# Decoder layer, attention stage: value projections moved into the position part and written by VectorE in the next block; first outputs normalised ahead of the last adds

## The reference, cut to what matters

```python
q, k, v = split_heads(x @ Wq + bq), split_heads(x @ Wk + bk), split_heads(x @ Wv + bv)   # 16 heads of 8
scores = einsum('bhqd,bhkd->bhqk', q, k) / scale
c2p = take_along_axis(einsum('bhqd,hpd->bhqp', q, pos_k), c2p_pos, -1)      # q against 64 position buckets
p2c = swapaxes(take_along_axis(einsum('bhkd,hpd->bhkp', k, pos_k), p2c_pos, -1), -1, -2)
probs = softmax(scores + (c2p + p2c) / scale)
out = einsum('bhqk,bhkd->bhqd', probs, v) @ Wo + bo + x
x = layernorm(x + layernorm(out) * ln_scale + ln_bias)
```

## Time and profile before

| | us |
|---|---|
| median of three runs | 2737.05 |
| the profiled execution's own time | 2735.33 |
| its span, first to last instruction | 2733.6 |
| TensorE busy | 2375.6 (87%) |
| ScalarE busy | 2270.4 (83%) |
| VectorE busy | 2129.8 (78%) |
| GpSimd busy | 577.6 (21%) |
| mean granted TensorE clock | 0.945 |

### The profile page before, as it was taken

The page is one execution under the profiler, slowest core; times in us unless marked ns, Lnnn a source line. Parts: engine busy times, 40 slices in busy tenths (PEclk is TensorE's granted clock), DMA queues, the critical chain, the costliest instruction groups (busy, mean ns, idle before and its releaser), DMA issues. The chain is left out here.

```text
span 2733.6 us, 64386 instructions
## 1 busy us (share of the span) xinstructions
PE 2375.6 (87%) x18133; PEld 1298.0 (47%) x18133; DVE 2129.8 (78%) x6451; ACT 2270.4 (83%) x4511; POOL 577.6 (21%) x435
## 2 busy tenths in 40 slices
PE   3888888888883478555999999999999999999997
PEld 2666665666662256233444444444444444444443
DVE  4778888788775766954788888888888888888886
ACT  2899999989993533266999999999999999999996
POOL 3233242332420011233111111111111111111114
PEclk6999999999996589876999999999999999999999
DMA  4231222312211000000111111111111111111112
GB/s 112 53 77 44 68 58 51 75 45 67 58 43 46 1 0 0 31 0 1 47 52 57 46 46 46 46 52 57 46 46 46 46 53 56 46 46 46 46 52 87
DMA packets 195627, 129.61 MB, mean 47 GB/s; under 512 B 26667, under 2 KB 184443, under 8 KB 195579
## 3 DMA queue, kind: packets, MB, share of 16 engines
q1 hardware_dynamic: 195579, 129.02, 17.9%
HBM read 78.10 MB, written 4.73 MB: 30 GB/s over the span
## 5 line engine op out<-in xcount | busy, mean ns | idle before, releaser
L2002 DVE TENSOR_TENSOR c_Hl<-c_HF,c_Hh 128x512 f16<-128x512 f32 x1028 | 679.4, 688 | 161.5 <-ACT c_Hh L1889 145.1
L1885 ACT ACTIVATE c_HF<-c_H,c_b 128x512 f32<-128x512 f32 x1028 | 710.6, 691 | 64.2 <-PE c_H L1824 44.0
L1889 ACT ACTIVATE c_Hh<-c_H,c_b 128x512 f16<-128x512 f32 x1028 | 706.2, 687 | 0.0
L1940 POOL TENSOR_TENSOR c_EX<-c_euler,c_D 128x16 f32<-128x16 f32 x65 | 188.7, 2902 | 1194.1 <-DVE c_D L1975 1194.1
L1823 PE MATMUL c_H<-c_Cl,SH 128*128 128x512 f16 x1028 | 390.2, 380 | 0.0
L1822 PE MATMUL c_H<-c_Ch,SH 128*128 128x512 f16 x1028 | 390.2, 380 | 0.0
L1824 PE MATMUL c_H<-c_Ch,SH 128*128 128x512 f16 x1028 | 390.0, 379 | 0.0
L1833 PE MATMUL c_Y<-c_Hh,SH 128*128 128x512 f16 x1024 | 388.1, 379 | 0.1
L1835 PE MATMUL c_Y<-c_Hl,SH 128*128 128x512 f16 x1024 | 388.1, 379 | 0.0
L1834 PE MATMUL c_Y<-c_Hh,SH 128*128 128x512 f16 x1024 | 388.1, 379 | 0.0
L649 ACT ACTIVATE a_E<-a_T,a_nm 128x128 f32<-128x128 f32 x1024 | 325.3, 395 | 27.6 <-DVE a_nm L741 26.2
(11 more groups left out here) (296 smaller groups left out, 4076.2 us busy)
## 6 DMA issues: line engine op xcount, KB each, us to landing
c_CWB<-c_rows SPq DMA_DIRECT2D x260, 256.0 KB, 4.0
a_AB<-a_ST SPq DMA_DIRECT2D x256, 128.0 KB, 2.4
a_QN<-a_QH SPq DMA_DIRECT2D x128, 32.0 KB, 1.9
a_KN<-a_KH SPq DMA_DIRECT2D x128, 32.0 KB, 1.9
out<-d_O SPq DMA_DIRECT2D x16, 256.0 KB, 2.3
a_QN<-a_QL SPq DMA_DIRECT2D x64, 32.0 KB, 1.9
a_KN<-a_KL SPq DMA_DIRECT2D x64, 32.0 KB, 1.9
CUR<-in_ctx SPq DMA_DIRECT2D x1, 1848.0 KB
```

Source lines behind the costliest of these rows:

```text
L1885: act.activation(HF[:, k % 4, :], bH[k % 4][:, :], ACT.Gelu_apprx_tanh, bias=b1[:, g % EXPERTS, f:f + 1], scale=1.0 / WSCALE).then_inc(hf_ ...
L1889: act.activation(Hh[:, g % 2, f, :], bH[k % 4][:, :], ACT.Gelu_apprx_tanh, bias=b1[:, g % EXPERTS, f:f + 1], scale=1.0 / WSCALE).then_inc( ...
L2002: dve.tensor_tensor(Hl[:, g % 2, f, :], HF[:, k % 4, :], Hh[:, g % 2, f, :], ALU.subtract)\
```

## The change

The four value projections move from steps 10 to 13 to steps 20 to 23, behind the two chunks of each step, and write bank bO in place of bM. VN and GpSimd's copy `values_out` go. `values_in` moves from u = 14 to u = 1 of the next block, and writes V itself, from the bank. TensorE's wait for VN ahead of the first `out_transpose` goes. The first `softmax_outputs`, at u = 15, comes ahead of that step's `add_positions`. The four unread matmuls write bE[0] in place of bO. In the prologue a memset of ET and a matmul that filled bO with zeros go.

```diff
--- before.py
+++ after.py
@@ -39,9 +39,9 @@
 TAIL = CHUNKS // 2
 NORM_STEPS = (2, 3, 4, 5, 6, 7, 14)
 TILE_STEPS = (5, 6, 7, 8, 9, 10, 11, 12)
-V_STEPS = (10, 11, 12, 13)
+V_STEPS = (20, 21, 22, 23)
 C2P_MID, P2C_MID = 47, 17
-CONSTS, FILLS, TAB, BUILT = 13, 6, 10, 4
+CONSTS, FILLS, TAB, BUILT = 13, 5, 10, 4
 DVE_CHUNKS = tuple((c, 1) for c in range(1, CHUNKS))
 ACT_CHUNKS = tuple((c, f) for c in range(CHUNKS) for f in range(2) if (c, f) not in DVE_CHUNKS)
 EARLY_MAX = range(0, 0)
@@ -162,7 +162,6 @@
         ST = sb("ST", [P, 2, 2, S, NG, NB], F16)
         AB = sb("AB", [P, 2, 2, S, NG * NB], F16)
         POS = sb("POS", [P, 2, ROWX, S])
-        VN = sb("VN", [P, NB, NH, DH])
         V = sb("V", [P, NB, NH, VCOLS])
         OC = sb("OC", [P, 2, UPB, S])
         T = sb("T", [P, 3, HG, S])
@@ -205,8 +204,7 @@
             sem(n) for n in ("loaded", "late_in", "x_in", "consts", "filled"))
         tab_ps, tab, built = sem("tab_ps"), sem("tab"), sem("built")
 
-        xb, xT_ps, xT_ok, vn_ok, v_ok, kd_ok = (
-            Count(sem(n), 1) for n in ("xb", "xT_ps", "xT_ok", "vn_ok", "v_ok", "kd_ok"))
+        xb, xT_ps, xT_ok, v_ok, kd_ok = (Count(sem(n), 1) for n in ("xb", "xT_ps", "xT_ok", "v_ok", "kd_ok"))
         v_ps = Count(sem("v_ps"), NB)
         qk_ps, hi_ok, lo_ok = (Count(sem(n), 2) for n in ("qk_ps", "hi_ok", "lo_ok"))
         qn_in, kn_in = ([Count(sem(n + str(g)), 16 * 3) for g in range(NG)] for n in ("qn_in", "kn_in"))
@@ -332,12 +330,6 @@
                                               group_mask[:, h:h + 1], 1.0, ALU.mult, ALU.mult)
                 last.then_inc(kd_ok.sem, 1)
 
-            def values_out(i, nxt):
-                if nxt:
-                    hold(pool, spare_pool, pv.sem, pv.at(i, UNITS))
-                hold(pool, spare_pool, vn_ok.sem, vn_ok.at(i, 1 + nxt))
-                pool.tensor_copy(V[:, :, :, 0:DH], VN[:, :, :, :]).then_inc(v_ok.sem, 1)
-
             n = 2
 
             def const(ins):
@@ -375,12 +367,9 @@
             pool.memset(V[:, :, :, :], 0.0).then_inc(filled, 1)
             pool.wait_ge(filled, 4)
             pool.memset(V[:, :, :, DH:DH + 1], 1.0).then_inc(filled, 1)
-            pool.wait_ge(filled, 5)
-            pool.memset(ET[:, 0, :, :], 0.0).then_inc(filled, 1)
             pool.wait_ge(filled, FILLS)
             pool.wait_ge(built, BUILT)
             spread_keys(0, 0)
-            values_out(0, 0)
             def power(i, n):
                 pool.wait_ge(var_ok.sem, var_ok.at(i, n + 1))
                 pool.tensor_tensor(rstd[:, :], rstd[:, :], half[:, :], ALU.pow).then_inc(rstd_ok.sem, 1)
@@ -405,7 +394,6 @@
                 residuals(i, first)
                 if not last:
                     spread_keys(i, 1)
-                    values_out(i, 1)
 
             body(0, first=True)
             with pool.Fori(1, NBLK - 1) as i:
@@ -432,7 +420,7 @@
                 pe.matmul(bG[1][:, :], Wk[:, :], xT[:, :, :], start=True, stop=True).then_inc(qk_ps.sem, 1)
 
             def project_v(b):
-                pe.matmul(bM[:, b * S:(b + 1) * S], xT[:, :, b], Wv[:, :], start=True, stop=True).then_inc(v_ps.sem, 1)
+                pe.matmul(bO[:, b * S:(b + 1) * S], xT[:, :, b], Wv[:, :], start=True, stop=True).then_inc(v_ps.sem, 1)
 
             def bucket_tile(i, nxt, n):
                 kind, g = n // NG, n % NG
@@ -509,8 +497,6 @@
 
             def out_transpose(i, b, last):
                 pe.wait_ge(on_ok.sem, on_ok.at(i, b + 1))
-                if b == 0 and not last:
-                    pe.wait_ge(vn_ok.sem, vn_ok.at(i, 2))
                 if b == 0 and last:
                     pe.wait_ge(r_ok.sem, r_ok.at(i, 0))
                 pe.transpose(bM[:, b * S:(b + 1) * S], On[:, b % 2, :], ident[:, :]).then_inc(ot_ps.sem, 1)
@@ -548,7 +534,6 @@
             last.then_inc(tab_ps, 1)
             pe.wait_ge(built, BUILT)
             pe.wait_ge(filled, FILLS)
-            pe.matmul(bO[:, :], ident[:, :], ET[:, 0, :, :], start=True, stop=True)
             for n in range(TILES):
                 bucket_tile(0, 0, n)
             for c in range(CHUNKS):
@@ -572,8 +557,6 @@
                         project_q(i, 1)
                     if u == 2 and not last:
                         project_k()
-                    if u in V_STEPS and not last:
-                        project_v(V_STEPS.index(u))
                     for n in tiles_of(u):
                         if not last:
                             bucket_tile(i, 1, n)
@@ -586,9 +569,11 @@
                     if u >= UNITS and not last:
                         for c in (2 * (u - UNITS), 2 * (u - UNITS) + 1):
                             position_chunk(i, 1, c)
+                    if u in V_STEPS and not last:
+                        project_v(V_STEPS.index(u))
                     if u == UNITS + TAIL - 1 and not last:
                         for _ in range(4):
-                            pe.matmul(bO[:, :], window[:, 0:P], table[:, 0:2, :, :].rearrange("p g k n -> p (g k n)"),
+                            pe.matmul(bE[0][:, :], window[:, 0:P], table[:, 0:2, :, :].rearrange("p g k n -> p (g k n)"),
                                       start=True, stop=True)
 
             body(0)
@@ -711,14 +696,11 @@
                 dve.scalar_tensor_tensor((QL, KL)[n][:, :], bG[n][:, :], (bq, bk)[n][:, :], (QH, KH)[n][:, :],
                                          ALU.add, ALU.subtract).then_inc(lo_ok.sem, 1)
 
-            def values_in(i, nxt):
-                dve.wait_ge(v_ps.sem, v_ps.at(i, NB * (1 + nxt)))
-                if nxt:
-                    dve.wait_ge(v_ok.sem, v_ok.at(i, 1))
-                dve.tensor_tensor(VN[:, :, :, :].rearrange("p b h d -> p b (h d)"),
-                                  bM[:, :].rearrange("p (b n) -> p b n", b=NB),
-                                  bv_all[:, :].rearrange("p (a n) -> p a n", a=1).to_broadcast([P, NB, H]),
-                                  ALU.add).then_inc(vn_ok.sem, 1)
+            def values_in(i):
+                dve.wait_ge(v_ps.sem, v_ps.at(i, NB))
+                dve.tensor_tensor(V[:, :, :, 0:DH], bO[:, :].rearrange("p (b h d) -> p b h d", b=NB, h=NH),
+                                  bv_all[:, :].rearrange("p (a h d) -> p a h d", a=1, h=NH).to_broadcast([P, NB, NH, DH]),
+                                  ALU.add).then_inc(v_ok.sem, 1)
 
             def split_rows(i, nxt, n):
                 kind, g = n // NG, n % NG
@@ -891,7 +873,8 @@
             last.then_inc(built, 1)
             for k in range(2):
                 low_half(0, 0, k)
-            values_in(0, 0)
+            dve.wait_ge(filled, FILLS)
+            values_in(0)
             dve.wait_ge(built, BUILT)
             for k in range(TILES):
                 split_rows(0, 0, k)
@@ -902,15 +885,17 @@
 
             def body(i, first=False, last=False):
                 for u in range(UNITS + TAIL):
+                    if u == OUT_NORM[0]:
+                        softmax_outputs(i, 0)
                     if u < UNITS:
                         add_positions(i, u)
-                    for b in range(NB):
+                    for b in range(1, NB):
                         if u == OUT_NORM[b]:
                             softmax_outputs(i, b)
                     if u in (2, 3) and not last:
                         low_half(i, 1, u - 2)
-                    if u == 14 and not last:
-                        values_in(i, 1)
+                    if u == 1 and not first:
+                        values_in(i)
                     if u in NORM_STEPS and not first:
                         norm_step(i - 1, NORM_STEPS.index(u))
                     for k in tiles_of(u):
```

## The result

The changed kernel takes 2824.62 us (median of four runs, 2823.47 to 2827.51) against 2737.09 in the same session: 1.032 times the time before, 95% interval 1.0308 to 1.0333. That is +88 us where +17.6 was forecast, and outside every rival. The profiled execution spans 2824.0 us. A memset of the stage behind the attention starts at 844.9 us before and at 935.9 after: 91 us arise inside the attention, and nothing behind it.

The account below looks back on a forecast made before the run. ScalarE was taken to pace the units, the TensorE-VectorE loop the position part, TensorE the next block's start. 15 position parts x 1.14 plus 0.5 gave +17.6 us; forecast 2754 us, range 2745 to 2762.

Parts of the forecast that it names:

- Part 5: GpSimd's copy and prologue: 0, the dropped matmul hidden behind a DMA wait; last block's reordering: +0.5 us once.
- Part 3: Projections entering steps 20 to 23: first three cost 0.57 us together, the fourth its full 0.57; +1.14 us per block.
- Rival 1: Position part: a projection costs no more than Wo's slot, 0.43 us; +0.86 per block, 2750.4 us; chance 0.19.
- Rivals 3: Last adds on the path, with a gain only as large as the cost, near 1.1 per block: 2737 us; chance 0.07.
- 4: Position part: each projection also delays VectorE's loop, all slots exposed, 15 x 2.28 + 0.5: 2771.7 us; chance 0.06.
- Part 1: Projections leaving steps 10 to 13 free 2.28 us of TensorE per block, but ScalarE sets the pace: gain 0.
- Part 2: Step 14 without VN, first outputs ahead of unit 15's add: chunk 0 still waits for the DMA; gain 0.
- rival 2: Units' last adds are on the path and chunk 0 moves earlier: -0.48 us per block, 2730.4 us; chance 0.08.
- Part 4: values_in at step 1, writing V in 0.69 to 1.38 us, fits VectorE's 1.37 us idle time: 0.

Follow-up runs that it names:

- the first experiment: Changed kernel with one idle VectorE instruction ahead of its block loop, which then begins at instruction 321: 2745.09 us, 1.0035 times before.
- the shifted kernel: Kernel before, with one semaphore credit moved from VectorE to GpSimd so that VectorE's loop begins at 320: 2790.8 us, 1.0198.
- start 420: Changed kernel with 100 more idle VectorE instructions in the prologue, ahead of the loop: 2761.18 us, 1.0092.
- start 404: Changed kernel with 84 idle VectorE instructions ahead of its loop, which occupies 404 to 705: 2777.84 us, one run.
- values alone: Changed kernel with VectorE's loop at 321 and the old order of first outputs and last add, so only the value projections move: 2748.7 us, 1.0048.
- the transfers of GpSimd: Changed kernel with one idle VectorE instruction, four of the last eight transfers into AB issued by GpSimd: 2739.94 us, 1.0017.
- starts 403, 449 and 400: Changed kernel with 83, 129 and 80 idle VectorE instructions ahead of its loop: 2748.42, 2749.8 and 2750.86 us, one run each.
- 533: Changed kernel with 213 more idle VectorE instructions ahead of its loop, which ends at 835: 2784.2 us, 1.0176.
- order alone: Kernel before with only the first softmax_outputs ahead of the add of unit 15, VectorE's loop still at 321: 2748.6 us, 1.0048.

## Why the prediction was wrong

**The step that failed** is in the sum: it has terms for engines, slots and waits, and none for the loading of VectorE's instructions. Part 5 put the prologue at "0" as far as its work on TensorE is hidden; but the edits to `values_in` and its waits there also changed the number of VectorE's instructions ahead of the loop, from 321 to 320. That one costs 2824.62 - 2745.09 = 79.5 us. Over the thirteen passes from 167.96 to 889.52 it can be split: unread matmuls to chunk 0 took 41.68 on average against 37.05 (4.63 each, 60 us), and the position part 55.50 - 41.68 = 13.82 against 12.45 (1.37 each, 18 us), together 78. Both shares hold clock. The heads' adds come 5.48 us behind the unread matmuls on average, 1.99 in the first experiment: 3.49 us late each, 45 us, is the stall itself (of the 4.40 at 285.97, for instance, 1.11 had been a wait for the scores). The delay then grows by another 1.1 us on the way to chunk 0, 15 us together, in passes whose clock all fell behind the head. It did not grow where the clock held there: 3.64 and 3.68 in the one such pass of the shifted kernel, 1.21 us at the head and 1.26 at chunk 0 at start 420, 4.14 - 1.99 = 2.15 and 2.14 at start 404. The last 18 us are the clock in the position part, which fell in ten of thirteen passes. The 1.5 us that remain are the loop's first pass, which has no stall and lost 1.4 us to the clock (a position part of 13.86). So about 45 us are VectorE's stall and some 33 the clock that goes with it. That the clock fell because TensorE stood idle is what the rows suggest; the idle time alone doesn't decide it, since behind equal ones it sometimes held.

**Part 3 was right in mechanism and mis-sized.** The forecast was +1.14 per block; without the stall it is 49.48 - 48.70 = +0.78 (values alone) and 49.50 - 48.70 = +0.80 (whole change). Beside chunk 0, forecast and measured: chunk 10 at 8.19 and 8.19, chunk 11 at 8.52 and 8.52, the second projection at 8.86 and 8.86, chunk 12 at 9.86 and 9.75, chunk 15 at 11.64 and 11.54, the unread matmuls at 12.55 and 12.45, the next scores at 13.63 and 13.31. The transposition's 0.20, which stood on no row, was right (310.26 to 310.46). Two terms were off: the slot with Wo, 311.70 to 312.02 = 0.32 here and 0.43 in the sum, and the unread matmuls, 314.72 to 315.58 = 0.86 here and 1.08 in the sum. I had taken the whole distance behind 311.46 of the earlier trace rows as their length, so in the kernel before the next scores waited 0.22 for something else. The rows point at VectorE's last copy: it ended at 312.26 and the scores came at 312.54, 0.28 later, and without the unread matmuls the scores name that copy as their releaser and come 0.23 behind it. So the reading that TensorE alone sets the next block there was wrong; in the changed kernel the matmuls end later and do set it. Leaving them out gained 0.31 and not 0.86, because the copy is the next bound. Rival 1, by its number (+0.86), came nearer than the forecast, but by its reason (a cheaper projection) it was wrong: the slot is 0.57. Rivals 3 (no change) and 4 (all slots exposed, 2.28 per block) are out by the same +0.80.

**Part 1** (gain 0): the tile copies on ScalarE have no idle time in the first experiment's blocks either. As forecast.

**Part 2** (gain 0): in the whole change, as forecast. Chunk 0 stood 37.05 us behind the unread matmuls with the new order and 37.04 with the old (302.27 - 265.23), there released by the DMA (with the new order the page names no releaser), and the idle time in front of it grew from 0.54 to 1.34 and 1.35. The arithmetic of issue and landing was right; rival 2 (2730.4 us) is refuted by it, and by the transfers of GpSimd, which did move chunk 0. But the same reordering put into the kernel before costs 12.3 us, through the clock and 0.27 per block. I had no term for an idle time that grows on TensorE: I let speak for the clock, which held there with 0.54. With the values moved, an idle time of 1.35 left the clock alone in all thirteen blocks. What decides is open; the rows differ in the 0.24 us behind chunk 1, and in that TensorE is less full there (busy for 10.32 of the 11.69 us of a position part, in the first experiment for 12.09 of 12.41).

**Part 4** (gain 0): the write into V took 0.69 us (230.65), as in one piece, at u = 1, and nothing waited for it.

**The sum for the rest.** 15 x 0.79 = 11.9, and 12.4 us measured for the values alone (2748.7 against 2736.3 before). The whole change with the loop in a good place measures +8.8; the 3.6 us between the two don't lie in the attention (both reach the next stage's memset at 856 us), and aren't explained. The same change at starts 403, 449 and 400 measured +11.6 to +13.1, in one run each. The range would have been met at its lower end by the kernel with the idle instruction; by the change itself it was missed by 63 us.

## What to carry to other kernels

When an edit changes the number of instructions ahead of a loop or in it, look at the instruction queue's packets and at "issue" idle time at the loop's head before anything else; here one instruction decided over 79 us, and one that does nothing gave them back. A forecast for such an edit should carry a rival for it, with a chance and the price of one stall per pass. And an idle time that grows on TensorE need not be free even where nothing waits for it: see what the clock does behind it, block by block.

## What the runs showed of the hardware

- A loop of 302 to 304 instructions on VectorE was loaded again in every pass at starts 320, 404, 420 and 533, and never at 321 (with either length), 400, 403 and 449: 25 or 26 packets against 90 to 92 of 8 KB, five more per pass, and one idle instruction decides between them at 320 and 321 and at 403 and 404. Lines of 128 instructions, three of them kept, is a model that fits them all, and starts 403 and 404 were called by it, one instruction apart; what the chip really holds isn't seen.
- The idle time at the head was 4.4 to 5.0 us at start 320 and 3.1 to 3.5 at 404 and 533 (1.1 us of it a wait for the scores that stood there anyway), and at 420 the head was late by 1.0 to 1.2. Start 320 lies in its first line with one instruction alone, 404 in its last with one alone. What sets the length was not tried.
- A transfer of 128 KB from SBUF to SBUF issued by GpSimd landed 3.6 us after its issue where four were issued in a row (3.1 where two were), by SyncE 2.4.
- The clock fell in ten of thirteen position parts behind an idle time of 1.8 to 2.3 us (changed kernel), in seven of thirteen behind 1.33 (order alone), in none behind 1.35 (values alone), and in one of thirteen behind 0.6 (shifted kernel before). Behind the block's head it fell in all thirteen passes of the changed kernel, where TensorE stood idle for 1.8 to 2.4 us, and in twelve of thirteen of the shifted one (2.2 to 2.8); at starts 404, 420 and 533, with 0.7 to 0.9, it held in all.
